# Three small re-orderings at the start of a four-sequence transformer kernel: warm-up products, key tiles, weight halves

## The reference: what is computed

```
adj  = s * cond * softmax(x) / sqrt(512);  diagonal = -inf
mask = 1 at the 5120 largest entries of adj, else 0
x    = x + mask
x1   = layernorm(x) * (1 + scale1) + shift1        # six vectors from cond @ ada_w
q,k,v = x1 @ qkv_w                                 # 16 heads of 128
x'   = x + gate1 * (softmax(q k^T / sqrt(128)) v @ out_w)
x''  = x' + gate2 * (gelu((layernorm(x') * (1 + scale2) + shift2) @ w1) @ w2)
out  = (x + mask) + x''
```

## Time and profile before

| | |
|---|---|
| median of 3 runs | 1547.49 us (1547.04 to 1548.23) |
| profiled execution | 1547.5 us, span of its instructions 1545.4 us |
| TensorE busy | 1498.5 us, 97% of the span |
| VectorE, ScalarE, GpSimd busy | 1108.8, 884.4, 424.3 us |
| chain that ended last | PE 92%, DVE 4% |

### The profile page before, as it was taken

The page is one execution under the profiler, slowest core; times in us unless marked ns, Lnnn a source line. Parts: engine busy times, 40 slices in busy tenths (PEclk is TensorE's granted clock), DMA queues, the critical chain, the costliest instruction groups (busy, mean ns, idle before and its releaser), DMA issues.

```text
span 1545.4 us, 22200 instructions
## 1 busy us (share of the span) xinstructions
PE 1498.5 (97%) x7181; PEld 1246.7 (81%) x7181; DVE 1108.8 (72%) x2574; ACT 884.4 (57%) x1631; POOL 424.3 (27%) x371
## 2 busy tenths in 40 slices
PE   1999999999999999999999999999999999999998
PEld 1878788889788888888878888888878888888987
DVE  7878888767796887876784887876786666664431
ACT  4656777765846566662753666663671655554340
POOL 6714555554021422331000432232000233222000
PEclk9999999999999999999999999999999999999999
DMA  7866899996767788775465887677455787785463
GB/s 294 304 262 191 234 217 274 268 238 241 260 245 245 171 195 207 208 189 182 169 228 212 202 213 198 153 212 206 165 231 191 191 218 160 200 211 161 181 238 118
DMA packets 338611, 327.65 MB, mean 212 GB/s; under 512 B 274848, under 2 KB 279104, under 8 KB 335424
## 3 DMA queue, kind: packets, MB, share of 16 engines
q1 hardware_dynamic: 338208, 325.91, 70.9%
q10 hardware_dynamic: 288, 0.33, 0.1%
HBM read 204.54 MB, written 54.54 MB: 168 GB/s over the span
## 4 chain that ended last, share of the span: by engine, by line
PE 92%; DVE 4%; ACT 1%; DVEq 1%; issue 1%; DMA 1%; POOL 0%; SPq 0%; ACTq 0%; POOLq 0%
PE bank L1417 28%; PE bank L1418 27%; PE bank L1419 27%; PE bank L1754 2%; PE bank L1649 1%; PE bank L1644 1%; PE bank L1645 1%; DVE tb L1028 1%; PE bank L1449 1%; PE bank L1760 1%; DVEq L1248 1%; PE bank L1471 1%; PE bank L1468 1%; PE bank L1467 1%; PE bank L1584 0%
## 5 line engine op out<-in xcount | busy, mean ns | idle before, releaser
L740 POOL CAST probT<-turned 128x1024 fp32r<-128x1024 f16 x256 | 259.9, 1053 | 675.4 <-PE bank L1419 356.2
L1417 PE MATMUL bank<-xT,w 128*128 128x512 f32 (+1 forms) x712 | 281.1, 395 | 0.0
L1418 PE MATMUL bank<-xT,w 128*128 128x512 f32 (+1 forms) x712 | 275.3, 387 | 0.0
L1419 PE MATMUL bank<-xT,w 128*128 128x512 f32 (+1 forms) x712 | 275.2, 387 | 0.0
L883 ACT ACTIVATE prob<-bank,nbias 128x512 f32<-128x512 f32 x256 | 176.2, 689 | 108.1 <-DVE nbias L1249 99.0
L1266 DVE SCALAR_TENSOR_TENSOR halves<-prob,rinv,halves 128x512 f16<-128x512 f32 x256 | 175.8, 749 | 23.9 <-ACT halves L890 23.9
L890 ACT ACTIVATE halves<-prob,rinv 128x512 f16<-128x512 f32 x256 | 163.8, 712 | 26.3 <-DVE rinv L1262 24.6
L1247 DVE TENSOR_REDUCE rowmax<-bank 128x1 f32<-128x512 f32 x256 | 174.4, 681 | 0.5 <-issue 0.5
L1419 PEld LDWEIGHTS bank<-xT,w 128*128 128x128 f32 x712 | 133.7, 188 | 27.7
L1417 PEld LDWEIGHTS bank<-xT,w 128*128 128x128 f32 x712 | 134.5, 189 | 24.8
L1418 PEld LDWEIGHTS bank<-xT,w 128*128 128x128 f32 x712 | 133.9, 188 | 24.6
(11 more groups left out here) (172 smaller groups left out, 3306.7 us busy)
## 6 DMA issues: line engine op xcount, KB each, us to landing
w<-split_weights SPq DMA_DIRECT2D x154, 1024.0 KB, 5.6
split_weights<-w SPq DMA_DIRECT2D x38, 1024.0 KB, 6.7
wraw<-weights_in SPq DMA_DIRECT2D x48, 512.0 KB, 4.6
split_weights<-xT SPq DMA_DIRECT2D x7, 1024.0 KB, 7.7
adaw<-ada_w_in SPq DMA_DIRECT2D x4, 1536.0 KB, 12.8
xr<-x_in SPq DMA_DIRECT2D x4, 1024.0 KB, 5.8
turned<-halves SPq DMA_TRANSPOSE x256, 3.4
split_weights<-qk SPq DMA_DIRECT2D x3, 1024.0 KB, 7.7
```

Of the source, the lines that this page charges most:

```text
L740: nc.gpsimd.tensor_copy(probT[:, :, :, i * P:(i + 1) * P].rearrange("p a j t -> p (a j) t"), turned_of(h)[:, i, :, :]).then_inc(widened, 1)
L1417: pe.matmul(dst, w_hi_ap, x_hi_ap, start=first, stop=False)
L1418: pe.matmul(dst, w_hi_ap, x_lo_ap, start=False, stop=False)
L1419: return pe.matmul(dst, w_lo_ap, x_hi_ap, start=False, stop=last)
```

## The change

It has three parts. The idle products are 27 and not 40. The four key tiles of the next sequence stand two in head 3 and two in head 4, where one stood in head 2, two in head 3 and one in head 4; and the first count, which followed the last key tile directly, now follows `qk_part` in every block (in blocks 1 and 2 that is where it was, behind one more key tile). And in head 3 of block 0 GpSimd makes all three low weight halves ahead of its four casts, where it made two ahead and one behind.

```
-                    for k in range(at, at + max(1, n - 1)):
+                    ahead = n if h == QUAD - 1 else max(1, n - 1)
+                    for k in range(at, at + ahead):
                         split_lo(k)
                     widen(0, h)
-                    for k in range(at + max(1, n - 1), at + n):
+                    for k in range(at + ahead, at + n):
                         split_lo(k)
...
                 elif h == 2:
                     topk_adj(t, 2, NT)
-                    topk_keys(t, 0, 1)
                 elif h == 3:
-                    topk_keys(t, 1, 3)
+                    topk_keys(t, 0, 2)
                 elif h == 4:
-                    topk_keys(t, 3, NT)
-                    start_level(t, 0)
+                    topk_keys(t, 2, NT)
...
                 if not last and not keys_first:
                     topk_under_head(b + 1, h)
+                if not last and h == FIRST_TOTAL - 1:
+                    start_level(b + 1, 0)
                 if h + QUAD < H:
                     v_part(b, h + QUAD)
...
-            for i in range(40):
+            for i in range(27):
                 pe.matmul(bank[7][:, :], w[:, 0, 0, 0:P], w[:, 0, 0, 0:T], start=True, stop=True)
```

## The result

| | median, us | lowest to highest | runs |
|---|---|---|---|
| before, beside it | 1547.91 | 1546.88 to 1548.51 | 20 |
| after | 1550.32 | 1548.39 to 1551.81 | 20 |

The ratio is 1.0017, with a 95% interval of 1.0011 to 1.0023: the change costs 2.4 us. Forecast were 1545.7 us and a range up to 1547.7; the time lies above it. The profiled execution of after is a quick one among its runs, 1548.97 us with a span of 1547.0; before had 1547.5 and 1545.4. So the trace shows 1.5 us of the loss, and the rest stands in runs that left no trace. What is on record of those is their mean granted clock: it reads 0.997 to 0.999 in all 20 runs of after.

The account below looks back on a forecast made before the run. The prediction took TensorE, 92% of the chain, as the bound, with gains only where it is held. It summed -2.37 - 0.25 + 0.8 = -1.8 us from 1547.5 to 1545.7 us, range 1543.9 to 1547.7.

Parts of the forecast that it names:

- Part 1: Start: 13 fewer idle products bring the mask from 103.30 to 100.93, a gain of 2.37 us (1.7 to 2.95).
- the sum: Whole kernel: -2.37 for the start, -0.25 for block 0, +0.8 for blocks 1 and 2, together -1.8 us.
- The two waits of the earlier trace: Block 0, TensorE: 1.8 us for GpSimd's weight half and 0.8 us for VectorE's low halves of q and k.
- Part 2, block 0: Head 3's stall goes, about 0.9 us; VectorE's output of head 3 comes 0.9 to 1.5 us earlier; head 4 about equal.
- Part 3: Block 0, GpSimd: third-half stall shrinks to about 0.4 us, a 2.6 us wait appears at attend(3); with part 2, gain 0.25.
- The bound of 4.67: Head 3, block 0: GpSimd's four casts take at most 4.67 us, where 4.01 was taken.
- The clock rival: After the start's idle products: slow clock while TensorE turns 8 tiles, products 0.41 us apart, about 1551 us; chance 0.04.
- the wait of 2.6 us: Block 0, attend(3): TensorE waits about 2.6 us for GpSimd's casts, in place of both earlier stalls.
- Blocks 1 and 2: First totals wait for VectorE's o_part(3) behind one more key tile: +0.5 and +0.3, together +0.8 us.
- the lower bound: Blocks 1 and 2: the added wait costs 0 if there is slack that the offsets hide.
- The casts' rival: Block 0: casts of 4.67, L1266 slower, count late, so about 1547.1 us; chance 0.15.
- The bounds of the terms: Whole kernel: the terms' limits were said to give -3.4 to -0.1, so 1544.1 to 1547.4 us.

Follow-up runs that it names:

- p1_only: The kernel before with 27 idle products for 40, nothing else: 1546.48 us, ratio 0.9993.
- p1_between: The kernel before with 27 idle products and, in head 3 of block 0, GpSimd's third half between third and fourth cast: 1546.18 us, ratio 0.9989.
- between_count: p1_between with the first count also moved to its head's end, keys as before: 1546.73 us, ratio 0.9994.
- thin_keys: After with GpSimd's order of head 3 as before, and the key tiles of head 4, block 0, on 8 of 512 columns: 1546.65 us, ratio 0.9993.
- none_only: The kernel before with no idle products at the start (0 for 40), all else as before: 1547.70 us, ratio 1.0002.
- undo_p3: After with GpSimd's order of head 3 as before; 27 idle products and the new key tiles and count stay: 1547.64 us, ratio 1.0.
- p2_only: The kernel before with the new place of the key tiles and first count, nothing else: 1548.80 us, ratio 1.0009.
- thin_halves: After with VectorE's low halves of the probabilities (L1265) in head 4, block 0, on 8 of 512 columns: 1547.32 us, ratio 1.0.
- undo_p1: After with 40 idle products again; the new key tiles, count and GpSimd order stay: 1551.62 us, ratio 1.0027.
- fill_wait: After with 12 unread products on TensorE ahead of the casts' wait at attend(3), block 0: 1547.84 us, ratio 1.0004.

## Why the prediction was wrong, step by step

*Part 1: right at the start, not to the end.* 27 products take 8.00 us, the mask starts at 100.55 (forecast 100.93), and the second rows come 2.75 us earlier, 2.3 without the 0.44 from ahead of the start, for the 2.37 of the sum. A part of it is the late start of before's one trace. And the sum let this gain run to the end. In p1_only 1.1 of 2.6 us went back within block 0, and in four others (p1_between, between_count, thin_keys, none_only) 0.8 to 1.1 us goes near 311 us. In p1_between ScalarE waits there 2.60 us for the transposed low halves, where it waited 0.72 before:

```profile
305.43 2.57 ACT L896 ACTIVATE halves<-prob,rinv 128x512 f16<-128x512 f32 x4 [2.60 <-DMA turned<-halves]
```

That row starts at 305.04 in before: these transposes land no earlier although the engines are ahead. What holds them was not tried and stays open. The two waits of the earlier trace rows were not all that bounds block 0: a chain hides what stands 1 us behind it.

*Part 2, block 0: half right.* The stall at head 3 went, worth 1.0 us (forecast 0.9). "In head 4 two tiles stand for one tile and the count, about equal" holds only while GpSimd is quiet beside them, as in after (0.42 and 0.69). Where it casts, they take 6.4 us (undo_p3). And the count of block 0, moved back, was put at nothing; in p2_only and undo_p3 the first total waits 0.34 us for `o_part(3)`.

*Part 3: here the prediction failed.* The place was as forecast, the stall for the third half shrank to 0.75 us (forecast 0.4) and the new wait came. But `attend(3)` starts at 185.20. The forecast 185.95 is in the time of before; with the start's 2.37 us off it is 183.6. On the curve that is -1.0 for -2.6: 1.6 us late, of which the casts are 1.35. Two steps failed.

The first is the choice "The new casts lie beside VectorE's L1266 and not beside key tiles, so I take 4.01". Beside it they take 5.36, and L1265 5.20 for 2.74 (thin_halves: 3.98 beside the same four instructions on 8 columns). The bound of 4.67 was too low as well: it came from a stretch in which only part of the casts had a neighbour. That rule of the Trainium skill, page "GPSIMD Engine Reference", section 1 (Specifications), on the SBUF interfaces shared by GpSimd and VectorE, bore on L1266 as much as on the key tiles. The trace agrees, and at twice the price that I gave it.

The second is that the wait was priced as idle time only. The clock rival was set at the start, where after's trace shows no fall, and the wait of 2.6 us that the same text forecast for `attend(3)` was not put to the same question. The clock fell behind it and cost 1.67 us in the trace, 2.5 in undo_p1's trace and 2.5 in the medians (fill_wait). The Trainium skill, page "TensorE: Matmul & The Clock Gate", Part 1, which I had cited for the start, holds for this place too: in its table an idle stretch puts the busy clock back to the lower level. The trace agrees (0.50 behind the wait). The wait of 2.4 us in thin_halves did so too. So the forecast was not consistent: its own 2.6 us were enough for the clock to fall.

*Blocks 1 and 2: right in kind.* ScalarE's count of block 1 begins 549.60 - 547.79 = 1.81 later in time, of which 0.8 is the offset of the whole. At TensorE's two totals the curve rises by 0.1 each, for 0.5 and 0.3: there was slack that the offsets hid, as the lower bound said.

*The rivals.* The casts' rival had the right place and too small a price (1547.1). The clock's rival had the right mechanism at the wrong place for after's trace. Its counter, that TensorE pauses between the rows at 107.91 and the modulation at 109.33 and keeps its pace, does not hold in every execution: in between_count's trace the clock fell at just that pause. The measured time is the two together at `attend(3)`, a case that I had not put down.

*The range.* The bounds of the terms do not add up to the -3.4 to -0.1 that stands there. They give -2.95 - 1.0 + 0 = -3.95 and -1.7 + 0.6 + 1.3 = +0.2. Even that upper end lies 2.2 us below the measured +2.4.

## What to carry to other kernels

When a reorder concentrates several short waits of TensorE into one, price the clock behind it too: here eight products at half pace, and a dozen unread products in the wait bought them back. One trace is one execution: read the clock of the other runs as well before you say that it did not fall. Before you move GpSimd's work, look at what VectorE does beside it in the new place, not in the old one, and take the price from a stretch where the two lie wholly side by side. Undo parts in pairs as well as alone, since one part's cost can hide another's.

## What the runs showed of the hardware

- VectorE and GpSimd slow each other down: four casts 4.01 to 5.36 us, four `scalar_tensor_tensor` 2.74 to 5.20 (after), two key tiles 2.5 to 6.4 (after, undo_p3). In thin_keys a VectorE instruction on 8 columns took 0.80 to 2.26 us, up to the end of GpSimd's own. This includes `tensor_scalar`, which has one tensor input (0.42 alone, 1.06 to 1.11 beside casts), so the case is wider than the instructions with two SBUF inputs that the prediction named.
- After idle stretches of 2.4 us (thin_halves) and 3.75 us (after) TensorE's clock was at half for 3.4 us, in undo_p1 after 3.74 us for 6.8; after 1.9 and 1.7 us with products between them (undo_p3) its trace shows no fall. It differs between executions: behind 0.50 and 1.34 us with eight products between, it fell in between_count's trace and not in p1_between's, and 9 of undo_p3's 11 runs have a mean clock of 0.998 or 0.999.
- With TensorE idle for 6.84 us at the start, the clock was back at full 5.7 us after the first work (none_only), and all that cost 0.7 us in the trace.
